# Half 0's row of reciprocal deviations: a DVE block turn and two DMAs over HBM in place of four TensorE transposes

## The chip, the cores and the metric

The kernel runs on one core of one Trainium2 chip. The metric is the device time of the core in microseconds (us). A core has five engines with a program of their own each: TensorE (PE in the profile; its weight loads are PEld), VectorE (DVE), ScalarE (ACT), GpSimd (POOL) and SyncE (SP), which here issues all DMAs. They meet at semaphores only.

## The reference, cut to what matters

Two blocks over x of (4, 256, 256), which is 1024 tokens of 256 features. Each adds to x what it makes of the normalised x:

```python
def _layernorm(x, axis=-1, eps=1e-05):
    return (x - mean) / sqrt(var + eps)
# block 1: one of 4 experts by token id, the same matrix W[e] three times
for e in range(4):
    g = silu(h @ W[e].T); u = h @ W[e].T
    y = (g * u) @ W[e].T            # W: ctx_2048
    out = where(expert_ids == e, y, out)
x = x + out
# block 2: routed mixture of 16 experts (top 4), and a shared expert
x = x + routed(h2) + shared(h2)     # h2 = _layernorm(x)
```

As gate and up use the same matrix, block 1 needs one product z = h W.T for both, silu(z) * z, and a second product.

## The kernel before, in words

The tokens are split into two halves of 512. Activations lie feature-major in SBUF: features on the partitions, tokens along the row, two blocks k of 128 features. A float32 product is made of three fp32r products, high by high, low by high and high by low, and sums in a PSUM bank of 128x512. So each expert takes six matmuls for one half and one block of output features.

Block 1 is eight "mixes" of four experts each, in the order of the list `mixes`: mixes 0 and 1 are the first product of half 0 (both output blocks), mix 2 the first product of half 1, block 0, and so on. The results of the four experts lie in a ring of six PSUM banks. For mix n, ACT copies expert 0's bank to `prod` (`first_z`, L494), and DVE then overwrites it, expert by expert, where the token's id is beyond a threshold (`pick`, L707, one copy_predicated of 128x512 each).

The layer norm of half 0 is split. `centre` subtracts only the mean, so that the matmuls can start early. As the division by the deviation is by token, it can come after the first product: `scale` (L668) multiplies the picked `prod` with `rstd_all`, the same row of 512 factors on all partitions. The factors are made by POOL's `rstd_of(0)` (L457, a power of -0.5), as 128 tokens on the partitions by 4 tiles. To make a row of them, `rstd_rows` on PE transposes each of the four columns, broadcast to 128x128, into bank 4 (L996), inside mix 1 behind its expert 0; ACT's `spread_rstd` (L517) copies the bank to `rstd_all`. Half 1 is normalised in full before its transposes (`layer_norm_apply(1)` on DVE, `apply_norm(1)` on ACT, then `norm_transposes("n1", 1, 1)` on PE inside mix 1 behind expert 1, L938). Its transposed banks are split into `xn_hi` (ACT, L487) and `xn_lo` (DVE, `x_low`, L686), which mix 2 reads: in `mix`, `operands(k, True)` waits for `xlo_done` ahead of the third matmul of each k.

The order on every engine is written out by hand; there is no planner. On DVE it is `thresholds(0)`, `pick(0, [1])`, `layer_norm_apply(1)`, `pick(0, [2, 3])`, `scale(0)`, `pick(1, [1, 2])`, two `x_low` of half 1, `hidden_product(0)`, and on.

The weights come in 15 pieces through four slots of `stage`, all issued by SP: `load_piece(n)` waits until piece n - 4 has been cast (`w_hi`) and its rest taken (`w_lo`). Pieces 0 to 3 are block 1's; 4 to 14 block 2's. SP issues, in order: the inputs, pieces 0 to 3 among them, ids, xt, bias; pieces 4 up to the last but two; then `write_rows(0)`, which sends the routing weights of half 0 over HBM in the manner that the change now uses for the deviations: a DVE block transpose (L791), a write to HBM (L374), a wait, and reads that broadcast a row to many partitions (L410).

Of the kernel before, what the change touches and what calls it, by code (L numbers as in the profile page):

```python
# [19 lines left out]
F32 = mybir.dt.float32  # L20
# [4 lines left out]
ALU = mybir.AluOpType  # L25
ACT = mybir.ActivationFunctionType
# [52 lines left out]
def build(nc, first_d, x_d, xt_d, ids_d, ctx_d, bias_d, gu_d, wd0_d, wd_d, out_d):  # L79
# [4 lines left out]
    with ExitStack() as ctx:  # L84
        def sb(name, shape, dt=F32):
            return ctx.enter_context(nc.sbuf_tensor(name, shape, dt))

        def sem(name):
            return ctx.enter_context(nc.semaphore(name))
# [12 lines left out]
        wd_lo = sb("wd_lo", [P, ITEMS, D], F32R)  # L102
        rstd_all = sb("rstd_all", [P, HALF])
        minus_mean = sb("minus_mean", [P, TT])
        warm = sb("warm", [P, HALF], BF16)
# [32 lines left out]
        xn_blocks = x[:, TT:].rearrange("p t d -> p (t d)").rearrange("p (m t i) -> p t m i", t=TT, i=LANES)  # L138
        xn_turn = xn[:].rearrange("p t d -> p (t d)").rearrange("p (k c) -> p k c", k=KC)
        x1_d = nc.dram_tensor("x1_d", (HALF, D), F32, kind="Internal").ap()  # L140
        xn_d = nc.dram_tensor("xn_d", (QUARTERS, KC, LANES, HALF), F32, kind="Internal").ap()
# [20 lines left out]
        dstep, astep = sem("dstep"), sem("astep")  # L162
        rstd_in, z_scaled = sem("rstd_in"), sem("z_scaled")
        h1_product = sem("h1_product")
        varied, powered, shifted = sem("varied"), sem("powered"), sem("shifted")
# [18 lines left out]

        side_order = [("n1", 0, 0, 4), ("n1", 0, 1, 5), ("rstd", 0, 0, 4), ("n1", 1, 0, 4), ("n1", 1, 1, 5),
                      ("x1", 0, 0, 4), ("x1", 0, 1, 5), ("n2", 0, 0, 4), ("n2", 0, 1, 5)]
        side_at = {u[:3]: n for n, u in enumerate(side_order)}

        def wait_side_read(eng, b, n):

            before = [u for u in side_order[:n] if u[3] == b]
            if not before:
                return
            what, h, k, _ = before[-1]
            if what in ("n1", "n2"):
                count = (HALVES * KC if what == "n2" else 0) + h * KC + k + 1
                eng.wait_ge(xhi_done, max(count, KC))
                eng.wait_ge(xlo_done, count)
            elif what == "rstd":
                eng.wait_ge(rstd_in, 1)  # L200
            else:
                eng.wait_ge(normed_v, (HALVES + 1) * TT // 2)
                eng.wait_ge(normed_a, (HALVES + 1) * TT // 2)
# [19 lines left out]
        def side_bank(what, h, c):  # L223
            return bank[side_order[side_at[what, h, c]][3]]
# [120 lines left out]
        def _(sp):  # L345
# [15 lines left out]
            sp.dma_start(xt[:], xt_d).then_inc(xt_in, 16)  # L361
            sp.dma_start(bias[:], bias_d.partition_broadcast(P)).then_inc(bias_in, 16)
            for n in range(SLOTS, len(pieces) - 2):
                load_piece(n)
# [70 lines left out]
        def _(pool):  # L435
# [18 lines left out]
            def rstd_of(n):  # L454

                pool.wait_ge(varied, n + 1)
                nc.gpsimd.tensor_tensor(rstd[:, n], vareps[:, n], power[:], ALU.pow).then_inc(powered, 1)  # L457

            nc.gpsimd.memset(comb[:], 0.0).then_inc(comb_zero, 1)
            for n in range(E1):  # L460
                low_part(n)
# [14 lines left out]
        def _(act):  # L476
# [27 lines left out]
            def apply_norm(n):  # L504
# [4 lines left out]
                for t in range(TT):  # L509
                    if t not in BY_VECTOR[n]:  # L510
                        nc.scalar.activation(xn[:, t], tile_to_norm(n, t), ACT.Identity, bias=shift[:, n, t:t + 1],
                                             scale=rstd[:, n, t:t + 1]).then_inc(normed_a, 1)

            def spread_rstd():

                act.wait_ge(side_done, side_at["rstd", 0, 0] + 1)
                nc.scalar.activation(rstd_all[:], side_bank("rstd", 0, 0)[:], ACT.Copy).then_inc(rstd_in, 1)  # L517

# [64 lines left out]
            first_z(0)  # L583
            spread_rstd()
            apply_norm(1)
# [45 lines left out]
        def _(dve):  # L631
# [23 lines left out]
            def centre(t):  # L655
# [6 lines left out]
                nc.vector.tensor_scalar(xn[:, t], x[:, t], meanvar[:, 0, t, 0:1], None, ALU.subtract).then_inc(normed_v, 1)  # L662

            def scale(n):

                dve.wait_ge(rstd_in, 1)
                dve.wait_ge(z_picked, (n + 1) * (E1 - 1))
                nc.vector.tensor_tensor(prod[:, n % 2], prod[:, n % 2], rstd_all[:], ALU.mult).then_inc(z_scaled, 1)  # L668
# [175 lines left out]
            layer_norm_vars(1)  # L844
            masked = [thresholds(0)]
            pick(0, masked[0], [1])
            layer_norm_apply(1)
            pick(0, masked[0], [2, 3])
            scale(0)
            pick(1, masked[0], [1, 2])  # L850
            x_low("n1", 1, 0)
# [66 lines left out]
        def _(pe):  # L918
# [71 lines left out]

            def rstd_rows():

                pe.wait_ge(powered, 1)
                b = side_wait("rstd", 0, 0)
                for t in range(TT):
                    ins = nc.tensor.transpose(b[:, t * P:(t + 1) * P], rstd[:, 0, t:t + 1].to_broadcast([P, P]), consts_sb[:, 0:P])  # L996
                ins.then_inc(side_done, 1)

            def first_mix():
# [100 lines left out]
            first_mix()  # L1100
            mix(1, {0: rstd_rows, 1: lambda: norm_transposes("n1", 1, 1)})
            for n in range(2, 5):
# [60 lines left out]
```

## Time and profile before

| | us |
|---|---|
| time, median of 3 runs | 171.73 |
| lowest, highest | 171.45, 172.15 |
| the profiled execution's own time | 171.54 |
| its span in the trace | 169.3 |
| outside the span | 2.24 |
| PE busy | 163.9 |
| DVE busy | 117.6 |
| ACT busy | 69.3 |
| POOL busy | 37.5 |

The span runs from the first instruction to the last that the trace holds. Busy times of different engines overlap. The matmuls are pipelined: one of 128x512 is shown as some 0.40 us long, while the next one starts 0.23 us behind it, so PE's pace is read from starts and not from lengths.

### The profile page before, as it was taken

Reading aid. Unit: us, or ns where it says so; the run is one execution under the profiler, and the core shown is the slowest. Engines: PE = TensorE matmul, PEld = TensorE weight load, DVE = VectorE, ACT = ScalarE, POOL = GpSimd, SP = SyncE. Lnnn points to the kernel's source line nnn. Section 1 sums busy time; section 2 is a strip of 40 time slices with the busy share of each in tenths; the row PEclk is TensorE's granted clock in tenths of the full one; section 3 lists DMA queues with packets and bytes.
Section 4 is the critical chain, followed back from the end, with each engine's and each line's share of the span. In section 5 each row is a group of like instructions: output and inputs, shape, how many; then the busy total and the mean of one; then the engine's idle time right before and its main releaser. Section 6 shows DMA issues by size and latency. Waiting matters only on the chain.

```text
span 169.3 us, 2188 instructions
## 1 busy us (share of the span) xinstructions
PE 163.9 (97%) x712; PEld 128.7 (76%) x712; DVE 117.6 (69%) x233; ACT 69.3 (41%) x117; POOL 37.5 (22%) x36
## 2 busy tenths in 40 slices
PE   6899999999999999999999999999999999999992
PEld 2478888788867888888888777888788888878881
DVE  0899699946994988888998875776934444444452
ACT  3832641751348354436642257634212222222220
POOL 2492000375700015670794000000000000000000
PEclk9999999999999999999999999999999999999999
DMA  5999000055440046979205520026362111100003
GB/s 174 302 389 324 25 2 0 0 142 229 124 124 6 11 122 160 286 229 232 84 13 124 157 91 0 4 49 214 123 189 61 66 62 62 62 2 0 4 0 124
DMA packets 11923, 18.50 MB, mean 109 GB/s; under 512 B 3624, under 2 KB 5896, under 8 KB 11784
## 3 DMA queue, kind: packets, MB, share of 16 engines
q1 hardware_dynamic: 11912, 18.36, 35.2%
q8 instruction: 6, 0.10, 0.2%
q14 instruction: 5, 0.04, 0.1%
HBM read 16.13 MB, written 2.23 MB: 108 GB/s over the span
## 4 chain that ended last, share of the span: by engine, by line
PE 94%; DMA 2%; DVE 2%; issue 1%; DVEq 0%
PE bank L971 23%; PE bank L1067 14%; PE bank L1065 13%; PE bank L1066 13%; PE bank L1085 7%; PE bank L1088 7%; PE bank L1086 7%; DMA first<-first_d 2%; PE bank L938 2%; PE bank L1012 1%; PE bank L1017 1%; PE bank L1062 1%; PE bank L1061 1%; PE bank L1007 1%; PE bank L950 1%
## 5 line engine op out<-in xcount | busy, mean ns | idle before, releaser
L1067 PE MATMUL bank<-xn_lo,gu_hi 128*128 128x512 f32 (+1 forms) x104 | 41.1, 395 | 0.0
L1065 PE MATMUL bank<-xn_hi,gu_lo 128*128 128x512 f32 x96 | 38.0, 396 | 0.0
L1066 PE MATMUL bank<-xn_hi,gu_hi 128*128 128x512 f32 x96 | 38.0, 396 | 0.0
L573 ACT ACTIVATE h_hi<-hid 128x512 fp32r<-128x512 f32 (+1 forms) x26 | 16.4, 632 | 48.7 <-DVE hid L818 48.7
L823 DVE TENSOR_TENSOR h_lo<-hid,h_hi 128x512 fp32r<-128x512 f32 (+1 forms) x26 | 19.0, 732 | 14.9 <-ACT h_hi L573 14.9
L1067 PEld LDWEIGHTS bank<-xn_lo,gu_hi 128*128 128x128 f32 (+1 forms) x104 | 19.4, 187 | 4.9
L707 DVE COPY_PREDICATED prod<-beyond,bank 128x512 f32<-128x512 uint8 x24 | 17.6, 739 | 6.7 <-PE bank L971 5.2
L563 ACT ACTIVATE act_sb<-bank 128x512 f32<-128x512 f32 (+1 forms) x26 | 15.3, 590 | 16.0 <-PE bank L1067 15.9
L1065 PEld LDWEIGHTS bank<-xn_hi,gu_lo 128*128 128x128 f32 x96 | 18.0, 188 | 4.4
L1066 PEld LDWEIGHTS bank<-xn_hi,gu_hi 128*128 128x128 f32 x96 | 18.0, 188 | 4.3
L451 POOL TENSOR_TENSOR gu_lo<-stage,gu_hi 128x512 fp32r<-128x512 f32 x12 | 17.2, 1454 | 17.6 <-ACT gu_hi L480 17.6
L1085 PE MATMUL bank<-h_hi,wd_lo 128*128 128x512 f32 (+1 forms) x52 | 20.6, 396 | 0.0
L1088 PE MATMUL bank<-h_lo,wd_hi 128*128 128x512 f32 (+1 forms) x52 | 20.6, 395 | 0.0
L1086 PE MATMUL bank<-h_hi,wd_hi 128*128 128x512 f32 (+1 forms) x52 | 20.5, 395 | 0.0
L818 DVE TENSOR_TENSOR hid<-prod,bank 128x512 f32<-128x512 f32 x24 | 16.5, 688 | 1.8
L805 DVE TENSOR_TENSOR prod<-act_sb,ids 128x512 f32<-128x512 f32 x12 | 10.3, 862 | 8.1 <-ACT act_sb L563 8.1
L805 DVE TENSOR_TENSOR prod<-act_sb,first 128x512 f32<-128x512 f32 x12 | 9.8, 818 | 6.0 <-ACT act_sb L563 5.2
L971 PE MATMUL bank<-h_hi,ctx_hi 128*128 128x512 f32 x32 | 12.8, 399 | 0.0
L971 PE MATMUL bank<-h_lo,ctx_hi 128*128 128x512 f32 x32 | 12.8, 399 | 0.0
L971 PE MATMUL bank<-h_hi,ctx_lo 128*128 128x512 f32 x32 | 12.7, 395 | 0.0
L1088 PEld LDWEIGHTS bank<-h_lo,wd_hi 128*128 128x128 f32 (+1 forms) x52 | 9.8, 188 | 2.4
L1086 PEld LDWEIGHTS bank<-h_hi,wd_hi 128*128 128x128 f32 (+1 forms) x52 | 9.8, 188 | 2.3
(96 smaller groups left out, 218.1 us busy)
## 6 DMA issues: line engine op xcount, KB each, us to landing
stage<-gu_d SPq DMA_DIRECT2D x6, 512.0 KB, 3.6
stage<-wd_d SPq DMA_DIRECT2D x3, 512.0 KB, 4.3
first<-comb_d SPq DMA_DIRECT2D x8, 192.0 KB, 2.7
ids<-comb_d SPq DMA_DIRECT2D x8, 192.0 KB, 2.9
stage<-ctx_d SPq DMA_DIRECT2D x4, 256.0 KB, 5.2
xt<-xt_d SPq DMA_DIRECT2D x1, 1024.0 KB, 9.7
first<-comb_d SPq DMA_DIRECT2D x8, 128.0 KB, 3.0
ids<-comb_d SPq DMA_DIRECT2D x8, 128.0 KB, 3.0
```

The lines of the kernel that those rows point to most:

```text
L451: ins = nc.gpsimd.tensor_tensor(lo[:, s], st[:, s], hi[:, s].bitcast(F32), ALU.subtract)
L707: nc.vector.copy_predicated(prod[:, n % 2], beyond[:, e - 1, h * HALF:(h + 1) * HALF], ring_bank("z", n, e)[:]).then_inc(z_picked, 1)
L805: nc.vector.tensor_tensor(prod[:, g % 2], act_sb[:, g % 2], rows, ALU.mult).then_inc(prod_done, 1)
L818: nc.vector.tensor_tensor(hid[0:w, g % 2], src, up_bank(g)[0:w, :], ALU.mult).then_inc(hid_done, 1)
L823: nc.vector.tensor_tensor(h_lo[0:w, slot[g]], hid[0:w, g % 2], h_hi[0:w, slot[g]].bitcast(F32), ALU.subtract).then_inc(hlo_done, 1)
L971: return nc.tensor.matmul(ring_bank("z", n, e)[:], (ctx_hi, ctx_lo)[a][:, e, k, f], parts[k][b], start=start, stop=stop)
L1065: nc.tensor.matmul(out[:], gu_lo[:, cols], xn_hi[:, h, k], start=(k == 0), stop=False)
L1066: nc.tensor.matmul(out[:], gu_hi[:, cols], xn_hi[:, h, k], start=False, stop=False)
L1067: ins = nc.tensor.matmul(out[0:rows, :], gu_hi[:, wide], xn_lo[:, h, k], start=False, stop=(k == KC - 1))
L1085: nc.tensor.matmul(acc[k][:], wd_lo[0:w, c, cols], hi, start=(c == 0), stop=False)
L1086: nc.tensor.matmul(acc[k][:], wd_hi[0:w, c, cols], hi, start=False, stop=False)
L1088: ins = nc.tensor.matmul(acc[k][:], wd_hi[0:w, c, cols], lo, start=False, stop=(c == ITEMS - 1))
```

## The change

The four transposes on PE, their side bank turn and ACT's copy go. POOL writes half 0's factors into columns 0 to 3 of a zeroed tile `deviation` of 128x32. DVE turns it in blocks of 32x32 (`turn_deviations`, behind `thresholds(0)`). SP writes the turned tile to HBM, waits for that, and reads the 512 factors back, broadcast to 128 partitions, into `rstd_all`; `scale` waits for this read. Pieces 4 and on are issued behind the read. On DVE, `scale(0)` now stands behind `pick(1, [1])` and ahead of `pick(1, [2])`.

```diff
@@ -101,6 +101,8 @@
         wd_hi = sb("wd_hi", [P, ITEMS, D], F32R)
         wd_lo = sb("wd_lo", [P, ITEMS, D], F32R)
         rstd_all = sb("rstd_all", [P, HALF])
+        deviation = sb("deviation", [P, LANES])
+        deviation_row = sb("deviation_row", [P, LANES])
         minus_mean = sb("minus_mean", [P, TT])
         warm = sb("warm", [P, HALF], BF16)
         ids = sb("ids", [P, TOKENS], I32)
@@ -137,6 +139,7 @@
         x1_blocks = x[:, TT:].rearrange("p t d -> p (t d)").rearrange("p (b k i) -> p k b i", k=KC, i=LANES)
         xn_blocks = x[:, TT:].rearrange("p t d -> p (t d)").rearrange("p (m t i) -> p t m i", t=TT, i=LANES)
         xn_turn = xn[:].rearrange("p t d -> p (t d)").rearrange("p (k c) -> p k c", k=KC)
+        rstd_d = nc.dram_tensor("rstd_d", (LANES, P), F32, kind="Internal").ap()
         x1_d = nc.dram_tensor("x1_d", (HALF, D), F32, kind="Internal").ap()
         xn_d = nc.dram_tensor("xn_d", (QUARTERS, KC, LANES, HALF), F32, kind="Internal").ap()
         comb_d = nc.dram_tensor("comb_d", (HALVES, LANES, HALF), F32, kind="Internal").ap()
@@ -182,7 +186,7 @@
         N = len(items)
         place = {item: g for g, item in enumerate(items)}
 
-        side_order = [("n1", 0, 0, 4), ("n1", 0, 1, 5), ("rstd", 0, 0, 4), ("n1", 1, 0, 4), ("n1", 1, 1, 5),
+        side_order = [("n1", 0, 0, 4), ("n1", 0, 1, 5), ("n1", 1, 0, 4), ("n1", 1, 1, 5),
                       ("x1", 0, 0, 4), ("x1", 0, 1, 5), ("n2", 0, 0, 4), ("n2", 0, 1, 5)]
         side_at = {u[:3]: n for n, u in enumerate(side_order)}
 
@@ -360,6 +362,10 @@
             sp.dma_start(ids[:], ids_d.partition_broadcast(P)).then_inc(ids_in, 16)
             sp.dma_start(xt[:], xt_d).then_inc(xt_in, 16)
             sp.dma_start(bias[:], bias_d.partition_broadcast(P)).then_inc(bias_in, 16)
+            sp.wait_ge(deviation_turned, 1)
+            sp.dma_start(rstd_d.rearrange("t (q i) -> q t i", i=LANES), deviation_row[:]).then_inc(rstd_out, 16)
+            sp.wait_ge(rstd_out, 16)
+            sp.dma_start(rstd_all[:], rstd_d[0:TT].rearrange("t c -> (t c)").partition_broadcast(P)).then_inc(rstd_in, 16)
             for n in range(SLOTS, len(pieces) - 2):
                 load_piece(n)
 
@@ -454,9 +460,11 @@
             def rstd_of(n):
 
                 pool.wait_ge(varied, n + 1)
-                nc.gpsimd.tensor_tensor(rstd[:, n], vareps[:, n], power[:], ALU.pow).then_inc(powered, 1)
+                nc.gpsimd.tensor_tensor(deviation[:, 0:TT] if n == 0 else rstd[:, n], vareps[:, n], power[:], ALU.pow).then_inc(powered, 1)
 
             nc.gpsimd.memset(comb[:], 0.0).then_inc(comb_zero, 1)
+            nc.gpsimd.memset(deviation[:], 0.0).then_inc(deviation_zero, 1)
+            pool.wait_ge(deviation_zero, 1)
             for n in range(E1):
                 low_part(n)
             rstd_of(0)
@@ -511,11 +519,6 @@
                         nc.scalar.activation(xn[:, t], tile_to_norm(n, t), ACT.Identity, bias=shift[:, n, t:t + 1],
                                              scale=rstd[:, n, t:t + 1]).then_inc(normed_a, 1)
 
-            def spread_rstd():
-
-                act.wait_ge(side_done, side_at["rstd", 0, 0] + 1)
-                nc.scalar.activation(rstd_all[:], side_bank("rstd", 0, 0)[:], ACT.Copy).then_inc(rstd_in, 1)
-
             def hidden_high(b):
                 act.wait_ge(h1_product, b + 1)
                 nc.scalar.activation(h_hi[:, b], hid[:, b % 2], ACT.Copy).then_inc(h1_high, 1)
@@ -581,7 +584,6 @@
             high_part(2)
             high_part(3)
             first_z(0)
-            spread_rstd()
             apply_norm(1)
             first_z(1)
             x_high("n1", 1, 0)
@@ -661,9 +663,14 @@
                 dve.wait_ge(dstep, steps[0])
                 nc.vector.tensor_scalar(xn[:, t], x[:, t], meanvar[:, 0, t, 0:1], None, ALU.subtract).then_inc(normed_v, 1)
 
+            def turn_deviations():
+
+                dve.wait_ge(powered, 1)
+                nc.vector.transpose(deviation_row[:], deviation[:]).then_inc(deviation_turned, 1)
+
             def scale(n):
 
-                dve.wait_ge(rstd_in, 1)
+                dve.wait_ge(rstd_in, 16)
                 dve.wait_ge(z_picked, (n + 1) * (E1 - 1))
                 nc.vector.tensor_tensor(prod[:, n % 2], prod[:, n % 2], rstd_all[:], ALU.mult).then_inc(z_scaled, 1)
 
@@ -843,11 +850,13 @@
                 tile_stats(1, t)
             layer_norm_vars(1)
             masked = [thresholds(0)]
+            turn_deviations()
             pick(0, masked[0], [1])
             layer_norm_apply(1)
             pick(0, masked[0], [2, 3])
+            pick(1, masked[0], [1])
             scale(0)
-            pick(1, masked[0], [1, 2])
+            pick(1, masked[0], [2])
             x_low("n1", 1, 0)
             x_low("n1", 1, 1)
             hidden_product(0)
@@ -988,14 +997,6 @@
                     if e in between:
                         between[e]()
 
-            def rstd_rows():
-
-                pe.wait_ge(powered, 1)
-                b = side_wait("rstd", 0, 0)
-                for t in range(TT):
-                    ins = nc.tensor.transpose(b[:, t * P:(t + 1) * P], rstd[:, 0, t:t + 1].to_broadcast([P, P]), consts_sb[:, 0:P])
-                ins.then_inc(side_done, 1)
-
             def first_mix():
 
                 z = [ring_bank("z", 0, e)[:] for e in range(E1)]
@@ -1098,7 +1099,7 @@
             norm_transposes("n1", 0, 0, (0, 2, 2, 1))
             keep_warm(3, HALF // 2)
             first_mix()
-            mix(1, {0: rstd_rows, 1: lambda: norm_transposes("n1", 1, 1)})
+            mix(1, {1: lambda: norm_transposes("n1", 1, 1)})
             for n in range(2, 5):
                 mix(n)
             mix(5, {1: lambda: (x1_transposes(0, 0), x1_transposes(0, 1))})
```

DVE, from the end of `thresholds(0)` to the first product of half 0's hidden values, before. The names: `beyond` is the mask, `bank1`, 6, 7 hold mix 0's experts 1 to 3, `bank3` and `bank0` mix 1's experts 1 and 2, `bank4` and `bank5` half 1's transposed features.

```order
L707 COPY_PREDICATED prod<-beyond,bank1 128x512
L673 SCALAR_TENSOR_TENSOR shift<-meanvar,rstd 128x4
L679 TENSOR_SCALAR xn<-first,meanvar,rstd 128x256 x2
L707 COPY_PREDICATED prod<-beyond,bank6 128x512
L707 COPY_PREDICATED prod<-beyond,bank7 128x512
L668 TENSOR_TENSOR prod<-prod,rstd_all 128x512
L707 COPY_PREDICATED prod<-beyond,bank3 128x512
L707 COPY_PREDICATED prod<-beyond,bank0 128x512
L686 TENSOR_TENSOR xn_lo<-bank4,xn_hi 128x512
L686 TENSOR_TENSOR xn_lo<-bank5,xn_hi 128x512
L715 TENSOR_TENSOR hid<-act_sb,prod 128x512
```

and now:

```order
L669 STREAM_TRANSPOSE deviation_row<-deviation 128x32
L714 COPY_PREDICATED prod<-beyond,bank1 128x512
L680 SCALAR_TENSOR_TENSOR shift<-meanvar,rstd 128x4
L686 TENSOR_SCALAR xn<-first,meanvar,rstd 128x256 x2
L714 COPY_PREDICATED prod<-beyond,bank6 128x512
L714 COPY_PREDICATED prod<-beyond,bank7 128x512
L714 COPY_PREDICATED prod<-beyond,bank3 128x512
L675 TENSOR_TENSOR prod<-prod,rstd_all 128x512
L714 COPY_PREDICATED prod<-beyond,bank0 128x512
L693 TENSOR_TENSOR xn_lo<-bank4,xn_hi 128x512
L693 TENSOR_TENSOR xn_lo<-bank5,xn_hi 128x512
L722 TENSOR_TENSOR hid<-act_sb,prod 128x512
```

The block turn stands ahead of everything else there, and the multiplication with `rstd_all` has moved from ahead of `bank3`'s pick to between `bank3`'s and `bank0`'s.

PE, from the end of mix 1's expert 0 (`bank2`) to the start of expert 1 (`bank3`), before:

```order
L971 MATMUL bank2<-xn_hi,ctx_hi 128x512
L971 MATMUL bank2<-xn_hi,ctx_lo 128x512
L971 MATMUL bank2<-xn_lo,ctx_hi 128x512
L996 MATMUL bank4<-first,rstd 128x128 x4
L971 MATMUL bank3<-xn_hi,ctx_hi 128x512
L971 MATMUL bank3<-xn_hi,ctx_lo 128x512
```

and now:

```order
L980 MATMUL bank2<-xn_hi,ctx_hi 128x512
L980 MATMUL bank2<-xn_hi,ctx_lo 128x512
L980 MATMUL bank2<-xn_lo,ctx_hi 128x512
L980 MATMUL bank3<-xn_hi,ctx_hi 128x512
L980 MATMUL bank3<-xn_hi,ctx_lo 128x512
```

The four transposes of `rstd` between the experts are gone; nothing else on PE moved.

SP, from the load of xt to the second weight piece of block 2, before:

```order
L361 DMA xt<-xt_d 128x2048
L362 DMA bias<-bias_d 128x16
L352 DMA stage<-gu_d 128x448
L352 DMA stage<-gu_d 128x1024
L352 DMA stage<-wd0_d 96x256
L352 DMA stage<-wd_d 128x1024
```

and now:

```order
L363 DMA xt<-xt_d 128x2048
L364 DMA bias<-bias_d 128x16
L366 DMA rstd_d<-deviation_row 4x32x32
L368 DMA rstd_all<-rstd_d 128x512
L354 DMA stage<-gu_d 128x448
L354 DMA stage<-gu_d 128x1024
L354 DMA stage<-wd0_d 96x256
```

Two DMAs stand between `bias` and the first `gu_d` piece, and every weight piece from 4 on is behind them. On ACT the only difference is that the copy to `rstd_all` (L517) is gone; on POOL one memset of 128x32 is new behind that of `comb`, and the first power writes `deviation`.

## Rows read from the trace of the kernel before

In the DMA rows, `x_d<-first` with a count of 4 is the write to the HBM tensor `x1_d`.

**Rows 1.** Page, part 1: busy time of each engine, share, instructions.

```profile
PE 163.9 (97%) x712; PEld 128.7 (76%) x712; DVE 117.6 (69%) x233; ACT 69.3 (41%) x117; POOL 37.5 (22%) x36
```

**Rows 2.** Page, part 4: the chain that ended last, shares by engine.

```profile
PE 94%; DMA 2%; DVE 2%; issue 1%; DVEq 0%
```

**Rows 3.** Windows: length, busy us of PE, PEld, DVE, ACT, POOL, PEclk, DMA, GB/s.

```profile
13.60:20.80 7.20, 7.20 (x38) 5.94 (x38) 5.37 (x10) 3.67 (x7) 0.06 (x1) 1.00 0.45 158
54.00:110.00 56.00, 56.00 (x242) 44.90 (x241) 46.45 (x104) 28.04 (x45) 18.55 (x13) 1.00 0.42 114
```

**Rows 4.** Timeline, PE, 15.0 to 16.0: start, length, engine, line, operation.

```profile
15.07 0.40 PE L971 MATMUL bank<-xn_lo,ctx_hi 128*128 128x512 f32 x1
15.30 0.60 PE L996 MATMUL bank<-first,rstd 128*128 128x128 f32 x4
...
15.97 0.40 PE L971 MATMUL bank<-xn_hi,ctx_lo 128*128 128x512 f32 x1
```

**Rows 5.** Timeline, PE and its weight loads, 20.8 to 21.8.

```profile
20.81 0.40 PE L971 MATMUL bank<-xn_hi,ctx_hi 128*128 128x512 f32 x1
...
21.04 0.19 PEld L971 LDWEIGHTS bank<-xn_lo,ctx_hi 128*128 128x128 f32 x1
21.27 0.40 PE L971 MATMUL bank<-xn_lo,ctx_hi 128*128 128x512 f32 x1
...
21.74 0.19 PEld L971 LDWEIGHTS bank<-xn_lo,ctx_hi 128*128 128x128 f32 x1
```

**Rows 6.** Timeline, DVE, 12.3 to 20.3.

```profile
12.31 1.15 DVE L693 TENSOR_SCALAR beyond<-ids 128x512 uint8<-128x512 int32 x3
...
16.57 0.69 DVE L668 TENSOR_TENSOR prod<-prod,rstd_all 128x512 f32<-128x512 f32 x1
18.03 0.74 DVE L707 COPY_PREDICATED prod<-beyond,bank 128x512 f32<-128x512 uint8 x1 [0.77 <-ACT prod L494]
19.61 0.74 DVE L707 COPY_PREDICATED prod<-beyond,bank 128x512 f32<-128x512 uint8 x1 [0.83 <-PE bank L971]
20.24 1.27 DVE L686 TENSOR_TENSOR xn_lo<-bank,xn_hi 128x512 fp32r<-128x512 f32 x2
```

**Rows 7.** Timeline, SP queue: bias; then, with DVE, the combine weights over HBM.

```profile
5.66 0.79 SPq L362 DMA_DIRECT2D bias<-bias_d  x1
...
57.02 0.31 DVE L791 STREAM_TRANSPOSE comb_row<-comb 128x128 f32<-128x128 f32 x1
57.36 0.67 SPq L374 DMA_DIRECT2D comb_d<-comb_row  x1
...
59.89 2.01 SPq L410 DMA_DIRECT2D first<-comb_d  x4
```

**Rows 8.** DMA issues: count, KB each, us from issue to landing (median).

```profile
first<-comb_d SPq DMA_DIRECT2D x1, 192.0 KB, 2.5
...
stage<-gu_d SPq DMA_DIRECT2D x6, 512.0 KB, 3.6
...
out_d<-xt SPq DMA_DIRECT2D x3, 256.0 KB, 2.1
...
x_d<-first SPq DMA_DIRECT2D x4, 128.0 KB, 3.1
...
first<-first_d SPq DMA_DIRECT2D x1, 320.0 KB, 3.2
...
bias<-bias_d SPq DMA_DIRECT2D x1, 8.0 KB, 9.3
```

**Rows 9.** Timeline, ACT, 15.9 to 17.5, and its first weight casts.

```profile
15.94 0.60 ACT L517 ACTIVATE rstd_all<-bank 128x512 f32<-128x512 f32 x1 [5.44 <-PE bank L996]
16.43 1.08 ACT L511 ACTIVATE xn<-first,shift,rstd 128x256 f32<-128x256 f32 x2
17.42 0.58 ACT L494 ACTIVATE prod<-bank 128x512 f32<-128x512 f32 x1
...
31.64 1.51 ACT L480 ACTIVATE gu_hi<-stage 128x448 fp32r<-128x448 f32 x2
```

More of the change, by code:

```diff
@@ L163, in build @@
         rstd_in, z_scaled = sem("rstd_in"), sem("z_scaled")
+        deviation_zero, deviation_turned, rstd_out = sem("deviation_zero"), sem("deviation_turned"), sem("rstd_out")
         h1_product = sem("h1_product")
@@ L198, in wait_side_read @@
                 eng.wait_ge(xlo_done, count)
-            elif what == "rstd":
-                eng.wait_ge(rstd_in, 1)
             else:
```

## The prediction

> **What bounds the kernel now.** I read the page first. PE is busy 163.9 of 169.3 us [rows 1] and holds 94% of the chain that ended last [rows 2]. The windows then show that PE is busy for all of the stretch around the change and of the long one behind it, at a granted clock of 1.00 [rows 3]. So the time is PE's instruction stream: what leaves it comes off the end, and what makes it wait is added, unless a wait downstream swallows it. The pace is read from starts, not lengths: 20.81 for one, 21.27 for the second behind it, so 0.23 us a matmul [rows 5].
>
> Next I read the timeline of PE around the transposes, and then looked for the next place where PE depends on DVE. It is mix 2, the first one to read half 1. Its third matmul reads the first `xn_lo` tile of half 1. The weight load for it started at 21.04, with the rest of PE, and its operand was the first of two DVE instructions from 20.24 on [rows 5, 6]. The pair takes 1.27 us, so one ends about 20.24 + 0.65 = 20.89. The slack is 0.15 us, of which some 0.05 are the semaphore's way: I call it 0.10. The second tile ends 21.51 for a load at 21.74 [rows 5, 6]: 0.23 us. So PE has no stall here now, but it has almost no slack against DVE either, and this is what the change must be read against.
>
> **What goes from PE.** Four transposes. The last matmul ahead of them starts at 15.07, they start at 15.30, and the second matmul behind them starts at 15.97 [rows 4]. Without them it would start two paces behind the first of these, at 15.53. That is 0.44 us. Everything on PE behind 15.3 comes 0.44 us earlier; the weight load of mix 2's third matmul would come at 20.60.
>
> **What goes from ACT.** The copy of 0.60 us, and with it the wait for the transposes. `apply_norm(1)` started at 16.43 behind it, and `first_z(1)`, which DVE's `pick(1, [1])` waited 0.77 us for, at 17.42 to 18.00 [rows 6, 9]. ACT will be free for both more than a microsecond earlier, so the pick can run when PE has finished its bank: six matmuls from 15.30 on, the last starting five paces later at 16.45 and ending 0.40 after, at about 16.9. The pick then runs to about 17.6. This is what makes the hole on DVE in which `scale(0)` is to sit: from about 17.6 until expert 2's bank is done, 19.61 - 0.44 = 19.17 [rows 6].
>
> **What is added on DVE.** One block turn of 128x32. The trace has one of 128x128 at 0.31 us [rows 7]; that is the upper bound, I take 0.2. It stands behind the thresholds, which end at 12.31 + 1.15 = 13.46 [rows 6], so the turn ends between 13.6 and 13.8; I take 13.7. The 0.2 us that it delays the picks lie beside PE's mix 1 and end in that hole: cost nothing. The memset on POOL falls in its idle time before the first weights are cast, and costs nothing either.
>
> **What is added on SP and the DMA queues.** A write of 16 KB, a wait, a broadcast read of 256 KB. The nearest thing in the trace is the same path for the combine weights: turn ends at 57.33, write issued at 57.36, first read issued at 59.89 [rows 7]. So 2.56 us from turned to read issued, with rows of 512 B where ours have 128 B. The read of 192 KB behind it, on empty queues, landed 2.5 us after its issue; one of 320 KB took 3.2 [rows 8]. For 256 KB I take 2.75. Sum: 13.7 + 2.56 + 2.75 + 0.05 = 19.06. For the shorter rows, and for what is left of the loads of xt and bias on the queues (bias, a mere 8 KB, landed 9.3 us after its issue because of what lay ahead of it [rows 8]), I add 0.15: `scale(0)` can start at about R = 19.2.
>
> Bounds for R. The write at its cheapest is an output write of 256 KB, 2.1 us, and the read is 2.5: 13.7 + 0.05 + 2.1 + 0.05 + 2.5 + 0.05 = 18.45. The write at its dearest is the one whose rows are 256 B, 3.1 us, and the read is 3.2 [rows 8]: 20.15.
>
> The Trainium skill, DMA: Bandwidth & Descriptors, section Anatomy of one DMA — SWDGE (gpsimd) path, puts a transfer at a fixed 2.0 us plus its bytes by 436 GB/s; for the two that would be an estimated 2.0 and 2.6 us, and R = 18.5. The trace's own 2.56 us and 2.5 for 192 KB stand at or above it, and the sum goes by the trace.
>
> **From R to PE.** A DVE instruction of 0.69 us hands on after about 0.62, the pick after 20.24 - 19.61 = 0.63 [rows 6]. With `scale(0)` at 19.2 the pick of expert 2 starts at 19.82 instead of 19.17, `xn_lo` at 20.45, its first tile is there at 21.10 and its weight load at 21.15, against 20.60. So PE waits 0.55 us. In general PE waits R - 18.65 (never below 0), and the second tile, with more slack, adds nothing. The net is R - 18.65 - 0.44 = R - 19.09: at R = 19.2 that is +0.1 us. Behind mix 2, DVE stands about 0.2 us later than before and PE 0.1 later, so I expect no new wait in the mixes that follow.
>
> **The queue behind the wait.** Behind `scale(0)` on DVE are the pick, both `xn_lo` and `hidden_product(0)`; PE waits for the middle two, ACT's `silu_z(0)` for `scale(0)` itself, with more room. Behind the two new DMAs on SP are weight pieces 4 to 7, which were issued right behind bias and would be now from about 16.7. One of 512 KB landed in 3.6 us; the four, at most 1.4 MB, should be there by 22 or so, and ACT first touches one at 31.64 [rows 8, 9]. Cost nothing; if that cover were gone, a late first piece would stop ACT and then PE one for one.
>
> **Sum.** 171.54 (profiled execution: span 169.3 and 2.24 around it) - 0.44 + 0.55 = 171.65. The median of the runs stands 0.19 above that execution, so I forecast 171.8.
>
> **Rivals.**
>
> Hidden: the two DMAs are faster than the combine path, R is under 18.65, and the full 0.44 us stays: 171.3. For it: the output write of 2.1 us, queues that the held-back pieces leave empty. Against it: the only such pair in the trace took 2.56 to the second issue. The Trainium skill's rule above is on this side.
>
> Slower: small rows. The write is made of 128 pieces of 128 B. The writes with 256 B rows took 3.1 us against 2.1 for an output write twice as large [rows 8]. If ours is like them or worse, and the read takes 3.2 us, R is 20.15, PE waits 1.50 in mix 2 and the net is +1.06: 172.8. It decides from R = 19.95, where the net passes +0.86. Against it: only 16 KB, and the transfers of 3.1 us were four behind each other. The Trainium skill, same page, Specifications, says that below 512 B a transfer is a read-modify-write; by that rule the write should stand above the combine path's, as here.
>
> Stuck behind xt: the row waits in the queues until the 1 MB of xt and bias is through. That is not later than bias's 5.66 + 9.3 = 15.0 us on the old schedule [rows 7, 8]; it could put 0.3 us more on R, which stays inside my own case.
>
> **Chances.** Net near zero, R from 18.65 to 19.95: 0.57, its own range 171.3 to 172.5. Hidden: 0.26. Slower: 0.14. Something that no row speaks of: 0.03. This kernel's measurement can't tell under 0.5%, 0.86 us, from no change. The hidden case is inside that, so the same: 0.57 + 0.26 less a little = 0.82. Slower 0.14. Faster 0.04, since no term is as large as 0.86 us. The range reaches from just under the hidden case, 171.2, to just short of the dearest, 172.7.
>
> **What would show it.** The block turn at 13.5, about 0.2 us long. The second DMA issued at 16.2 to 16.5, landed by 19.2. `scale(0)` idle before it, released by a DMA. PE's third matmul of mix 2 late by half a microsecond with its load released by `xn_lo`; everything behind mix 2 shifted by one constant of about +0.1 us. `first_z(1)` near 16. It is wrong if the PE has no gap in mix 2 (hidden), if the gap is over 1.3 us (slower), or if the shift at mix 2 isn't the shift at the end.

## The result, and the profile after

| | us |
|---|---|
| the kernel before, median of 15 runs (lowest, next to highest, highest) | 171.78 (171.39, 172.78, 329.26) |
| the changed kernel, median of 15 runs (lowest, highest) | 172.76 (172.01, 173.81) |
| ratio, 95% interval | 1.0042 (1.0024 to 1.0059) |
| profiled execution of the changed kernel: time, span | 172.80, 170.7 |

The one run of 329.26 us does not move the median. By the ratio the changed kernel is 0.42% or 0.7 us slower (0.4 to 1.0), which is inside the 0.5% that was called the same; 171.73 times the ratio is 172.5, inside the range of 171.2 to 172.7. By the medians it is 0.98 us or 0.57% slower, and the median of 172.76 lies 0.06 above the range. Either way the forecast of +0.1 us was low. The two profiled executions are 1.26 us apart: that of the kernel before was 0.24 below its median, that of the changed kernel 0.04 above.

The page, parts 1 and 4, answers to [rows 1] and [rows 2]:

```profile
PE 163.6 (96%) x708; PEld 128.2 (75%) x708; DVE 117.9 (69%) x234; ACT 68.9 (40%) x116; POOL 37.7 (22%) x37
PE 85%; DMA 7%; POOL 2%; DVE 1%; ACT 1%; SPq 1%; issue 1%; DVEq 0%
```
PE has 0.3 us less to do and holds 9 points less of the chain of work that ended last; DMAs have come into it. The windows (columns as in [rows 3]) say where:

```profile
13.60:20.80 7.20, 7.20 (x36) 5.69 (x34) 4.24 (x11) 2.66 (x5) 1.25 (x2) 1.00 0.44 116
20.80:26.40 5.60, 3.97 (x18) 3.14 (x18) 5.40 (x9) 2.47 (x4) 0.00 (x0) 1.00 0.43 155
54.00:110.00 56.00, 56.00 (x242) 44.89 (x241) 46.01 (x99) 28.91 (x46) 18.55 (x13) 1.00 0.43 114
```
PE is still full in the stretch with the change and in the long one behind. The stretch from 20.8 to 26.4 is the one that is not: 1.6 us of it are idle, at a granted clock of 1.00. The timeline of PE shows the gap [rows 4, 5]:

```profile
14.97 0.40 PE L980 MATMUL bank<-xn_lo,ctx_hi 128*128 128x512 f32 x1
15.21 0.40 PE L980 MATMUL bank<-xn_hi,ctx_hi 128*128 128x512 f32 x1
...
20.52 0.40 PE L980 MATMUL bank<-xn_hi,ctx_lo 128*128 128x512 f32 x1
22.55 0.50 PE L980 MATMUL bank<-xn_lo,ctx_hi 128*128 128x512 f32 x1 [1.63 <-DVE xn_lo L693]
22.88 0.39 PE L980 MATMUL bank<-xn_hi,ctx_hi 128*128 128x512 f32 x1
```
Behind the matmul at 14.97 the next expert starts one pace later at 15.21: the transposes and their 0.44 us are gone. At the third matmul of mix 2 PE stops for `xn_lo`: it starts at 22.55, where it would have been at 20.52 + 0.23 = 20.75. That is 1.80 us. The idle time of 1.63 in brackets is shorter, as it counts from the modelled end of the matmul ahead. Following the releaser back, DVE [rows 6]:

```profile
12.90 1.08 DVE L700 TENSOR_SCALAR beyond<-ids 128x512 uint8<-128x512 int32 x3
14.06 0.21 DVE L669 STREAM_TRANSPOSE deviation_row<-deviation 128x32 f32<-128x32 f32 x1
...
15.61 2.19 DVE L714 COPY_PREDICATED prod<-beyond,bank 128x512 f32<-128x512 uint8 x3
20.59 0.69 DVE L675 TENSOR_TENSOR prod<-prod,rstd_all 128x512 f32<-128x512 f32 x1 [2.79 <-DMA rstd_all<-rstd_d]
21.20 0.72 DVE L714 COPY_PREDICATED prod<-beyond,bank 128x512 f32<-128x512 uint8 x1
21.81 1.27 DVE L693 TENSOR_TENSOR xn_lo<-bank,xn_hi 128x512 fp32r<-128x512 f32 x2
```
The block turn takes 0.21 us. It started behind two things that ended almost together: the thresholds at 13.98, and POOL's power, which made the factors, at 14.02:

```profile
12.77 1.25 POOL L463 TENSOR_TENSOR deviation<-vareps,power 128x4 f32<-128x4 f32 x1
```
The three picks end at 17.80, and then `scale(0)` waits 2.79 us for the DMA; the pick and `xn_lo` follow at their usual spacing of 0.61. ACT, as forecast, has `apply_norm(1)` and `first_z(1)` 1.3 us earlier than in [rows 9]:

```profile
15.09 1.09 ACT L519 ACTIVATE xn<-first,shift,rstd 128x256 f32<-128x256 f32 x2 [4.36 <-DVE shift L680]
16.09 0.57 ACT L502 ACTIVATE prod<-bank 128x512 f32<-128x512 f32 x1
```
Last the SP queue and the landing of the read [rows 7, 8]:

```profile
14.30 0.68 SPq L366 DMA_DIRECT2D rstd_d<-deviation_row  x1
16.36 0.34 SPq L368 DMA_DIRECT2D rstd_all<-rstd_d  x1
16.81 0.83 SPq L354 DMA_DIRECT2D stage<-gu_d  x2
```
```profile
rstd_all<-rstd_d SPq DMA_DIRECT2D x1, 256.0 KB, 4.2
```
From the end of the turn, 14.27, to the issue of the read, 16.36, are 2.09 us. The read lands 4.2 us after its issue, at 20.56, and `scale(0)` starts at 20.59. The weight pieces are issued 0.45 us behind the read.

The whole difference is in this one gap: the matmul behind it starts at 22.88, against 21.51 before, +1.37:

```profile
21.51 0.40 PE L971 MATMUL bank<-xn_hi,ctx_hi 128*128 128x512 f32 x1
```
The transposes of x1 start at 41.77, against 40.41 before, +1.36; the spans differ by 1.4.

### The profile page after: what moved, and what is told of

The parts are those of the page before. It is cut to its first block, busy times and chain, and to the rows that moved or that the text cites. A ratio compares the mean times of both kernels' runs of the same rounds, so it can differ in the third digit from the quotient of the medians.

```text
span 170.7 us, 2183 instructions
## 1 busy us (share of the span) xinstructions
PE 163.6 (96%) x708; PEld 128.2 (75%) x708; DVE 117.9 (69%) x234; ACT 68.9 (40%) x116; POOL 37.7 (22%) x37
## 3 DMA queue, kind: packets, MB, share of 16 engines
HBM read 16.39 MB, written 2.24 MB: 109 GB/s over the span
## 4 chain that ended last, share of the span: by engine, by line
PE 85%; DMA 7%; POOL 2%; DVE 1%; ACT 1%; SPq 1%; issue 1%; DVEq 0%
PE bank L980 20%; PE bank L1068 14%; PE bank L1067 13%; PE bank L1066 13%; PE bank L1089 7%; PE bank L1086 7%; PE bank L1087 7%; DMA stage<-ctx_d 4%; DMA rstd_all<-rstd_d 2%; POOL ctx_lo L453 1%; DMA rstd_d<-deviation_row 1%; ACT ctx_hi L488 1%; PE bank L1063 1%; PE bank L1062 1%; POOL deviation L463 1%; PE bank L947 1%
## 5 line engine op out<-in xcount | busy, mean ns | idle before, releaser
L457 POOL TENSOR_TENSOR gu_lo<-stage,gu_hi 128x512 fp32r<-128x512 f32 x12 | 17.2, 1452 | 17.6 <-ACT gu_hi L488 17.6
```

Source lines behind the costliest of these rows:

```text
L457: ins = nc.gpsimd.tensor_tensor(lo[:, s], st[:, s], hi[:, s].bitcast(F32), ALU.subtract)
```

## Experiments

Twelve kernels, each against the kernel before on the same chip. The interval behind each ratio is a 95% interval. What they tell apart is why the read takes 4.2 us, and whether a late row has to cost anything.

**1. Weight pieces held until the read has landed.**

```diff
+            sp.wait_ge(rstd_in, 16)
             for n in range(SLOTS, len(pieces) - 2):
                 load_piece(n)
```

> The changed kernel, with weight pieces 4 and on held back until the broadcast read of the row has landed. Theory (contention): the read took 4.2 us because the four weight pieces issued right behind it share the 16 DMA engines; alone it lands in about 2.8 us, scale(0) starts near 19.2, PE's wait in mix 2 shrinks from 1.8 to about 0.5 us, and the time is that of the kernel before, within 0.2 us. Rival (the read itself is slow, 128 partitions reading one 2 KB row): the landing stays at 4 us or more and the time stays 1 us above the kernel before.

Measured: 171.66 us, ratio 0.9985 (0.9965 to 1.0005). The landing, then SP, DVE and PE:

```profile
rstd_all<-rstd_d SPq DMA_DIRECT2D x1, 256.0 KB, 3.0
```
```profile
16.01 0.34 SPq L368 DMA_DIRECT2D rstd_all<-rstd_d  x1
19.07 0.69 DVE L676 TENSOR_TENSOR prod<-prod,rstd_all 128x512 f32<-128x512 f32 x1 [1.54 <-DMA rstd_all<-rstd_d]
20.40 0.40 PE L981 MATMUL bank<-xn_hi,ctx_lo 128*128 128x512 f32 x1
21.04 0.50 PE L981 MATMUL bank<-xn_lo,ctx_hi 128*128 128x512 f32 x1 [0.25 <-DVE xn_lo L694]
```
The read lands in 3.0 us, `scale(0)` starts at 19.07 and PE waits 21.04 - 20.63 = 0.41 us, which is what R - 18.65 gives, 0.42. So the pieces behind the read are part of its 4.2 us.

**2. Pieces 4 to 7 ahead of both DMAs.** The loop over pieces 4 to 7 stands ahead of `sp.wait_ge(deviation_turned, 1)`.

> The changed kernel, with pieces 4 to 7 issued ahead of the two DMAs, as in the kernel before. The write then stands behind 1.3 MB in the queues, which run full until about 17 us. Theory (contention): the write lands at about 17.3 and the read, with nothing behind it, takes 2.8: scale(0) at about 20.3, the time close to the changed kernel's. Rival (the read itself is slow): 4 us and more for the read, scale(0) at 21.7 or later, over 1 us slower than the changed kernel.

Measured: 173.05 us, ratio 1.0067 (1.0044 to 1.0090).

```profile
rstd_all<-rstd_d SPq DMA_DIRECT2D x1, 256.0 KB, 3.3
```
The write now took 3.5 us from issue to the read's issue, 14.09 to 17.54, behind full queues. The read, with nothing behind it, took 3.3, and PE waited 2.24 us in mix 2. Between the two expectations, nearer to that of sharing. The time cannot be told from that of the changed kernel (1.0024 to 1.0059), so the order of the pieces and the pair decides nothing by itself; holding the pieces back, as in experiment 1, does.

**3. The read from rows of its own, with the pieces behind it and held.** Half 0 is then multiplied by weights and not by its factors; these two kernels only time the read.

```diff
-            sp.dma_start(rstd_all[:], rstd_d[0:TT].rearrange("t c -> (t c)").partition_broadcast(P)).then_inc(rstd_in, 16)
+            sp.dma_start(rstd_all[:], gu_d[:, 0:HALF]).then_inc(rstd_in, 16)
```

> The changed kernel with the broadcast read replaced by a read of the same 256 KB from 128 rows of their own (2 KB each, of the weights), so half 0 is multiplied by weights and not by its deviations. Weight pieces right behind it as in the changed kernel. Theory (sharing the engines with the pieces is the cause): it lands in 4 us or more too. Rival (128 descriptors on one row of HBM are slow and the pieces make it worse): under 3.3 us.

> The same read from rows of their own, with the weight pieces held back until it has landed; the held broadcast took 3.0 us. Theory of sharing alone: 2.8 to 3.0 us. Rival (one row is slow): 2.2 to 2.5 us, like the other unshared transfers of 256 KB.

Measured, one execution each, the first with the pieces behind it, the second with them held:

```profile
rstd_all<-gu_d SPq DMA_DIRECT2D x1, 256.0 KB, 2.7
```
```profile
rstd_all<-gu_d SPq DMA_DIRECT2D x1, 256.0 KB, 2.6
```
As many bytes from 128 rows of their own land in 2.7 us with the pieces right behind, against 4.2 from one row. Sharing alone is not the cause; my theory for the first experiment was half of it. The windows of 18 to 19 us, of the changed kernel and of the first of these two (the last numbers are DMA share and GB/s):

```profile
18.00:19.00 1.00, 1.00 (x6) 0.82 (x5) 0.00 (x0) 0.65 (x2) 0.00 (x0) 1.00 0.92 156
```
```profile
18.00:19.00 1.00, 1.00 (x7) 0.84 (x6) 0.34 (x2) 0.83 (x2) 0.00 (x0) 1.00 1.00 359
```
These windows mix the read with pieces (the read from rows of its own is over at 18.9). The windows of 17 to 18 us with the pieces held do not, the broadcast of experiment 1 first, then the read from rows of its own:

```profile
17.00:18.00 1.00, 1.00 (x8) 0.92 (x7) 0.54 (x1) 0.54 (x2) 0.00 (x0) 1.00 0.48 172
```
```profile
17.00:18.00 1.00, 1.00 (x10) 0.96 (x9) 0.74 (x1) 0.21 (x1) 0.00 (x0) 1.00 0.71 221
```
So alone the broadcast moves less while the engines are busy for half of the time. Its packets are not slow ones: the traces record each packet, and the median packet of 2 KB takes 84 ns in both kernels. They follow one another more slowly, over 1.77 us (16.99 to 18.76) against 1.35 (16.77 to 18.12). With the pieces behind it is 2.93 us (17.33 to 20.26) against 1.39 (17.14 to 18.53), the pieces' packets starting at 18.22 and 17.93. The median packet of the broadcast took 128 ns then, but 81 ns in experiment 6's first kernel, where the read took 4.3 us all the same. Why the packets of a broadcast come more slowly, and how the pieces make it worse, is not shown. The four cases together:

| landing, us | pieces right behind | pieces held |
|---|---|---|
| 128 reads of one 2 KB row | 4.2 (and 4.3, 4.4, 4.2 in three other kernels) | 3.0 |
| 128 rows of their own | 2.7 | 2.6 |

**4. Eight copies of the row.** POOL's power writes the four columns eight times, so that HBM holds eight rows of 2 KB, and partition p reads row p mod 8.

```diff
-            sp.dma_start(rstd_all[:], rstd_d[0:TT].rearrange("t c -> (t c)").partition_broadcast(P)).then_inc(rstd_in, 16)
+            sp.dma_start(rstd_all[:], rstd_d.rearrange("(r t) c -> r (t c)", t=TT).partition_broadcast(P // (LANES // TT))).then_inc(rstd_in, 16)
...
+                    c8 = deviation[:].rearrange("p (c t) -> p c t", t=TT)
+                    nc.gpsimd.tensor_tensor(c8, vareps[:, 0].unsqueeze(1).to_broadcast([P, LANES // TT, TT]),
+                                            power[:].unsqueeze(1).to_broadcast([P, LANES // TT, TT]), ALU.pow).then_inc(powered, 1)
```

> The changed kernel, with POOL writing the four columns of factors eight times over, so that the HBM tensor holds eight copies of the row (2 KB each) and neighbouring partitions read different copies; same bytes, weight pieces right behind as in the changed kernel. Theory (many reads of one 2 KB row at once are what is slow, and pieces behind them make it worse): the landing falls from 4.2-4.4 to 2.7-3.0 us, scale(0) starts near 19, PE waits 0 to 0.4 us in mix 2, the time is 0 to 0.5 us under the kernel before. Rival (it is the same small region of HBM, 16 KB, that counts, or freshly written data, and not the one row): 3.5 us or more, and 0.3 to 0.7 us slower than the kernel before.

Measured: 175.98 us, ratio 1.0224 (1.0180 to 1.0268). A miss of mine, since the edit changed a second thing. POOL, and the landing:

```profile
12.12 5.42 POOL L465 TENSOR_TENSOR deviation<-vareps,power 128x32 f32<-128x32 f32 x1
...
rstd_all<-rstd_d SPq DMA_DIRECT2D x1, 256.0 KB, 3.1
```
The power over 32 columns takes 5.42 us, the one over 4 about 1 to 1.25, so the turn came at 17.6. The landing is 3.1 us with the pieces behind, near the theory's 2.7 to 3.0 and below the rival's 3.5. One more thing differs: SP spends 0.60 us on issuing this read instead of 0.34, and the pieces go out 0.72 us behind its start instead of 0.45. What part of the gain is the copies' and what part the later pieces' is not told apart. The same with the late order of experiment 6:

> Eight copies, and scale(0) behind both x_low with the pick of expert 3 ahead of hidden_product(0). Theory (with the late order nobody waits for the row anyway): the same as the late order alone, -0.3 to -0.6 us against the kernel before, an earlier row buys nothing more. Rival: an earlier row shortens something else, -0.8 us or more.

Measured: 175.55 us, ratio 1.0191 (1.0148 to 1.0234). It decided nothing on the order, as the turn was late here too, and its profile has a price that the others do not show. Windows, columns as in [rows 3]:

```profile
16.00:19.00 3.00, 1.00 (x6) 0.55 (x4) 1.62 (x6) 0.60 (x2) 2.17 (x2) 1.00 0.03 4
19.00:22.50 3.50, 3.50 (x13) 3.01 (x13) 2.00 (x4) 2.06 (x5) 0.00 (x0) 0.51 0.41 121
22.50:30.00 7.50, 7.50 (x34) 5.99 (x33) 6.67 (x11) 2.46 (x4) 0.00 (x0) 1.00 0.49 166
```
PE stood idle for 2 of the 3 us up to 19, and the granted clock of the next 3.5 us is 0.51, the 1.2 GHz level, before it is back at 1.00. Such an idle stretch did not always bring it: in the profile of this experiment's first kernel PE waited 2.36 us up to 19.18 and the clock stayed at 1.00. Of the six executions here, the one with a mean granted clock of 1.00 took 173.94 us, the five with 0.99 took 174.78 to 175.85.

**5. Eight copies, made by a small DVE instruction.** The power is 128x4 again; DVE copies it eight times side by side (0.17 to 0.18 us) ahead of the turn. The four columns have a tile of their own, `dev4`, of 16 bytes a partition.

> The changed kernel with eight copies of the row in HBM, the copies made by a small DVE instruction (128x32 from 128x4) and the power on POOL as small as before (128x4). In the run with the power over 128x32 it took 5.4 us, which hid the test. Theory (many reads of one row are slow): block turn 0.3 us later than in the changed kernel, landing 3.1 us as in that run, so scale(0) at 19.3 to 19.7 against 20.59; PE waits 0.5 to 0.9 us in mix 2 and the time is 0 to 0.4 us above the kernel before. Rival (the read was faster there only because it came later, on quieter queues): landing 4 us or more, the time of the changed kernel or above.

Measured: 170.47 us, ratio 0.9892 (0.9853 to 0.9930), faster than either theory. The row:

```profile
20.50 0.69 DVE L680 TENSOR_TENSOR prod<-prod,rstd_all 128x512 f32<-128x512 f32 x1 [2.33 <-DMA rstd_all<-rstd_d]
...
rstd_all<-rstd_d SPq DMA_DIRECT2D x1, 256.0 KB, 3.7
```
In this execution the turn ended at 14.73, the read was issued at 16.8 and landed in 3.7 us: better than 4.2, worse than 3.1, and R is hardly earlier. PE waited 1.6 us in mix 2. The gain is not from the row; see below.

**6. The order on DVE.** First `scale(0)` behind both `x_low` of half 1:

```diff
-            scale(0)
             pick(1, masked[0], [2])
             x_low("n1", 1, 0)
             x_low("n1", 1, 1)
+            scale(0)
             hidden_product(0)
             pick(1, masked[0], [3])
```

> The changed kernel, with scale(0) on DVE behind both x_low of half 1, so that nothing that PE needs in mix 2 stands behind the DMA wait. Theory (the whole loss is that wait passed on through DVE's order): PE's wait at the third matmul of mix 2 goes, the row lands as late as before; scale(0) runs at about 21.1, hidden_product(0) about 1 us later than before, and PE waits 0 to 0.4 us at mix 3 instead; net -0.44 to 0 us against the kernel before. Rival (the late row costs the same wherever scale(0) stands, as the hidden values are late by as much): PE waits 1 us or more at mix 3 and the time stays near that of the changed kernel, +0.7 to +1.2 us.

Measured: 171.77 us, ratio 0.9985 (0.9963 to 1.0008). PE had no wait in mix 2 and one of 0.16 us at mix 3. In the profiled execution it also waited 0.48 us for `hid` at 93.8, far behind the change. The profiles of experiments 8 (0.42), 4 (0.78, first kernel), 5 (0.91) and 9 (0.21) have that wait too; those of the kernel before, of the changed kernel and of experiments 1, 2 and 7 do not. From the transposes of x1 to the last matmul it is 125.99 us here and 125.97 in experiment 8, against 125.3 in the kernel before and the changed one, so the wait costs some 0.7. What brings it is open. Then with `pick(1, masked[0], [3])` moved up between `scale(0)` and `hidden_product(0)`:

> The changed kernel with scale(0) on DVE behind both x_low of half 1, and the pick of mix 1's expert 3 between scale(0) and hidden_product(0), where DVE waited 0.7 us for ACT in the run with scale(0) late. Theory (only the order behind the wait costs; the hidden chain of half 0 has about 1.2 us of slack to mix 3): the row lands near 20.5 and nobody waits for it, hidden_low(1) ends about 0.3 us later than in the kernel before instead of 1.3, PE waits neither in mix 2 nor at mix 3, net -0.44 us against the kernel before, as without any row. Rival (a late row costs wherever it is waited for): PE waits 0.2 us or more at mix 3 and the time is that of the kernel before or above.

Measured: 171.34 us, ratio 0.9971 (0.9950 to 0.9992). DVE's timeline:

```profile
20.39 1.27 DVE L693 TENSOR_TENSOR xn_lo<-bank,xn_hi 128x512 fp32r<-128x512 f32 x2
21.58 0.68 DVE L675 TENSOR_TENSOR prod<-prod,rstd_all 128x512 f32<-128x512 f32 x1
22.18 0.73 DVE L714 COPY_PREDICATED prod<-beyond,bank 128x512 f32<-128x512 uint8 x1
22.96 0.69 DVE L722 TENSOR_TENSOR hid<-act_sb,prod 128x512 f32<-128x512 f32 x1
...
26.14 0.69 DVE L734 TENSOR_TENSOR h_lo<-hid,h_hi 128x512 fp32r<-128x512 f32 x1
```
The read took 4.4 us here and landed at 20.4; `scale(0)` at 21.58 did not wait. The last line is `hidden_low(1)`, ending at 26.83 against 26.14 before, and PE waited nowhere behind the first mix. From the first matmul of mix 1 to the transposes of x1 it is 26.07 us, against 26.51 in the kernel before and 27.96 in the changed one. The late row costs nothing.

**7. The price of what was removed.** No transposes, no copy, no row; `rstd_all` is ones.

> The kernel before without the four transposes and the copy; rstd_all is a row of ones set by POOL at the start, so half 0 is not divided by its deviation. The price of what the change removes, with nothing put in its place. Theory: PE's stream is the time, so -0.44 us against the kernel before. Rival (ACT's freed 0.6 us and the earlier picks count too): a gain over 0.7 us. Second rival (the transposes lay in slack): no gain.

Measured: 171.48 us, ratio 0.9971 (0.9949 to 0.9993), so -0.50 us (-0.88 to -0.12); the medians differ by -0.29. That rules out no gain, and does not tell 0.44 from 0.7. The profile does: from the first matmul of mix 1 to the transposes of x1 it is 26.08 us (14.28 to 40.36) against 26.51 before (13.90 to 40.41), so -0.43. The spans of the two profiled executions are both 169.3, since this one started mix 1 0.38 us later. The ratio is that of the late order with its row.

**8. The transposes kept, their bank unused.**

> The changed kernel with the four transposes still made on PE, into bank 4, where nobody reads them; the row still comes over HBM. Theory (in the changed kernel the DMA row sets when mix 2 goes on, so PE's stream ahead of it has over a microsecond of slack): PE waits 0.44 us less in mix 2 and the time is that of the changed kernel, +0.7 to +1.0 us against the kernel before. Rival (what is taken from PE counts in full and something else was added): 0.44 us slower than the changed kernel, +1.1 to +1.5 us.

Measured: 173.01 us, ratio 1.0066 (1.0044 to 1.0088), +1.1 us (0.8 to 1.5). PE:

```profile
16.24 0.60 PE L1007 MATMUL bank<-first,deviation 128*128 128x128 f32 x4
...
22.00 0.40 PE L982 MATMUL bank<-xn_hi,ctx_lo 128*128 128x512 f32 x1
22.73 0.50 PE L982 MATMUL bank<-xn_lo,ctx_hi 128*128 128x512 f32 x1 [0.33 <-DVE xn_lo L695]
```
By the profile the theory holds: the transposes are there, and PE waits 22.73 - 22.23 = 0.50 us in mix 2 instead of 1.80. This execution also started mix 1 1.03 us late (14.84 against 13.81), and its `scale(0)` 0.18 late (20.77). The sum fits: 1.80 - 0.44 - 1.03 + 0.18 = 0.51. The transposes of x1 start 0.19 later than in the changed kernel; the other 0.7 us by which this profiled execution is longer are the wait at 95.3, named in experiment 6. The time itself lies in the rival's range of +1.1 to +1.5, with an interval that reaches well into the theory's. I count the times as not deciding.

**9. Eight copies by DVE and the late order.**

> The same with scale(0) behind both x_low and the pick of expert 3 ahead of hidden_product(0). Theory (in the late order nobody waits for the row): -0.3 to -0.6 us against the kernel before, as the late order alone; the 0.3 us more on DVE lie in its idle time. Rival (what stands ahead of layer_norm_apply(1) on DVE is near PE's transposes too): 0.2 us or more slower than the late order alone.

Measured: 168.11 us (168.02 to 168.67), ratio 0.9779 (0.9746 to 0.9811). This beats both kernels by 2%, several times more than all that the row and the transposes have to give. The kernels of experiments 5 and 9 differ in the order on DVE alone, and were measured on one chip: 170.47 against 168.11, so here too the late order gains, 2.4 us. Of that, PE's wait in mix 2 is 1.6 and the wait named in experiment 6 is 0.7 longer in experiment 5.

## Why the prediction was right, and where it was off

What bounds the kernel: right. PE's stream is the time, what left it came off (0.44 forecast; with nothing in its place 0.43 by the profile, 0.50 with 0.12 to 0.88 by the times), and the wait that was added went through to the end unchanged, +1.37 us at mix 2 and +1.4 in the span.

The place of the new wait: right. The third matmul of mix 2 waits for `xn_lo`, held up through `scale(0)`. The formula, R - 18.65, gave 0.42, 2.23 and 1.94 us for starts of 19.07, 20.88 and 20.59; measured were 0.41, 2.24 and 1.80. The late order, with nothing else changed, took the loss away, so it was DVE's order that passed it on. No new wait stood behind it. Holding back the pieces cost ACT nothing.

R: forecast 19.2, measured 20.59. Term by term, in the profiled execution: the turn ended 0.57 us later than the 13.7 that I took, because this execution got x later (statistics of half 1 at 10.90 against 10.38), which moved the thresholds and POOL's power alike. The power ended last, 0.04 behind the thresholds, and the prediction had not asked when it would be done. The write and wait were 0.47 faster than the combine path's 2.56; the read took 4.2 for 2.75, +1.45; and the 0.15 that I had added for short rows and a full queue was not needed. Together +1.40. The read's time is the term that was mis-sized. My bounds for it were 2.5 and 3.2 us, taken from one row read by 96 partitions and from 320 KB of rows of their own. Neither showed a broadcast with half a megabyte queued right behind it. I had named the pieces behind the read as something that delays the pieces, and never asked what they do to the read.

By its own sign the prediction fails here. It called itself wrong, in the slower direction, if the gap was over 1.3 us, and the gap is 1.80; R is above 19.95, from where it counted the slower case, and above 20.15, its dearest, and +1.36 is more than the dearest net of +1.06. So the profiled execution landed in the size of a case that was given 0.14. That the ratio still lies inside the range is in part luck: the interval's upper end of 1.0 us is close to the range's, and the median is past it.

The slower rival had the right size (R from 19.95 on) but the wrong mechanism: it put the time on the write with its 128 B rows, and the write was quick, 2.09 us with its wait. The Trainium skill's fixed 2.0 us plus bytes (DMA: Bandwidth & Descriptors, Anatomy of one DMA — SWDGE (gpsimd) path), which the page gives for DMAs issued by GpSimd while SP issues these, fits the write (2.06 us from issue to the read's issue, an estimated 2.0) and the rows of their own (2.6 and 2.7, an estimated 2.6), but not the broadcast (3.0 and 4.2); its rule on transfers below 512 B (same page, Specifications) did not show in a write of 16 KB.

Net: by the profile +1.36 us, by the medians +0.98, by the ratio +0.7 (0.4 to 1.0). The rest is spread between executions, 172.0 to 173.8 for the changed kernel, and the forecast of +0.1 was between 0.3 and 0.9 us too low by the ratio.

## What to carry to other kernels

Where a result comes back late over DMA, first look at what stands behind the wait on the waiting engine: to put the wait behind what the bounding engine needs next was worth all of the loss, whatever the DMA did. In this kernel one row of 2 KB broadcast to 128 partitions was a transfer of its own kind: count such a one slower than its bytes, and keep bulk loads from right behind it. Spreading it over copies shortened it too, though not shown apart from the later pieces. To price a transfer, take a row of the trace with the same kind of source and with the same neighbours in the queue, not only with the same bytes.

## What the runs showed of the hardware that I had not expected

**One row read many times.** 4.2 to 4.4 us against 2.7 for as many bytes from rows of their own, both with the pieces behind; 3.0 against 2.6 with nothing queued behind. A packet took no longer (84 ns for both with nothing behind); the packets came more slowly. With eight copies 3.1 and 3.2 us in the two kernels with the late turn, and 3.7 and 3.2 in experiments 5 and 9.

**POOL's power** takes 5.42 us for 128x32 and 1.0 to 1.26 for 128x4.

**A faster matmul.** The kernels of experiments 5 and 9 have another pace of PE in all of their mixes. Matmuls of the last kernel near 60 us:

```profile
59.85 0.39 PE L1072 MATMUL bank<-xn_hi,gu_hi 128*128 128x512 f32 x1
60.08 0.39 PE L1073 MATMUL bank<-xn_lo,gu_hi 128*128 128x512 f32 x1
60.30 0.39 PE L1071 MATMUL bank<-xn_hi,gu_lo 128*128 128x512 f32 x1
```
They start 0.227 us apart instead of 0.233, at a granted clock of 1.00 in both. Over some 640 matmuls a difference of 0.006 us is 3.8 us, near the gain of 3.9 us; in experiment 5 PE's waits in mix 2 and at 94 take some of it back. The kernel before kept its time on the same chip (172.03), so it isn't the chip. Of what differs from the kernels with eight copies by POOL, one thing reaches every mix: `dev4` moves all SBUF tiles declared behind it, the moving operands `xn_hi`, `xn_lo`, `h_hi` and `h_lo` among them, while the weights lie where they lay. So I take the address of the moving operand as the cause. This is argued, not shown: no kernel was run that changes the address alone, the traces do not hold the addresses, and they say nothing of which addresses are good. The warm-up matmuls, whose tile `warm` moves as well, do not follow it: eight of them take 3.22 us in the last kernel, but 3.60 in that of experiment 5, 3.59 in the kernel before and 3.44 in the changed one. For the same reason the ratios of experiments 5 and 9 against the kernel before say nothing on copies or order; only their difference from each other does.
